# Weight chunks' low halves in parts, roots in two parts, router items ahead of the scores

## What is computed

```
xn = layernorm(x)                                  # (4, 512, 256)
q, k, v = xn @ Wq, xn @ Wk, xn @ Wv                # 16, 4, 4 heads of 128
q, k = rope(q) * scale, rope(k) / scale
s = softmax(causal(q @ k.T / sqrt(128))) @ v @ Wo
p = softmax(xn @ gate_w.T); w, idx = top_k(p, 2)
y = sum_e w_e * swiglu(xn @ w_gate_up[e]) @ w_down[e] + swiglu(xn @ shared_gate_up) @ shared_down
out = x + s * silu(y)
```

## Time and profile before

| | us |
|---|---|
| median of 3 runs (lowest, highest) | 685.43 (684.39, 685.63) |
| the profiled execution | 680.79 |
| its span | 678.9 |
| TensorE busy | 648.1 |
| VectorE busy | 545.6 |
| GpSimd busy | 533.9 |
| ScalarE busy | 421.5 |

### The profile page before, as it was taken

The page is one execution under the profiler, slowest core; times in us unless marked ns, Lnnn a source line. Parts: engine busy times, 40 slices in busy tenths (PEclk is TensorE's granted clock), DMA queues, the critical chain, the costliest instruction groups (busy, mean ns, idle before and its releaser), DMA issues.

```text
span 678.9 us, 15700 instructions
## 1 busy us (share of the span) xinstructions
PE 648.1 (95%) x5187; PEld 463.9 (68%) x5187; DVE 545.6 (80%) x1644; ACT 421.5 (62%) x1157; POOL 533.9 (79%) x609
## 2 busy tenths in 40 slices
PE   8888999999999999999999999999999999999994
PEld 6555677767676677666666766776667777777772
DVE  6999999999999999999899999999875454333356
ACT  5566777776575656666555756557677755555542
POOL 4899898898768787898989898898888974555544
PEclk9999999999999999999999999999999999999998
DMA  9980001011600000000000001000062735676874
GB/s 299 347 235 2 1 1 33 10 25 25 169 1 1 1 1 1 1 18 33 33 24 24 24 24 40 8 32 2 2 101 75 216 64 117 144 152 142 221 285 137
DMA packets 70816, 52.11 MB, mean 77 GB/s; under 512 B 41376, under 2 KB 64128, under 8 KB 70752
## 3 DMA queue, kind: packets, MB, share of 16 engines
q1 hardware_dynamic: 66688, 40.83, 22.8%
q0 software_dynamic: 3792, 10.43, 4.9%
q10 hardware_dynamic: 272, 0.02, 0.0%
HBM read 24.75 MB, written 18.77 MB: 64 GB/s over the span
## 4 chain that ended last, share of the span: by engine, by line
PE 42%; POOL 23%; DVE 19%; issue 8%; ACT 7%; DVEq 0%; ACTq 0%; POOLq 0%
POOL arena L638 11%; PE bank L1753 10%; PE bank L1787 6%; PE bank L1548 5%; PE bank L1608 5%; POOL arena L626 4%; PE bank L1579 4%; PE bank L1625 4%; PE bank L1592 4%; ACT arena L929 3%; POOL xs_dram L697 3%; DVE arena L1267 3%; DVE arena L1240 3%; POOL arena L631 3%; DVE arena L1239 2%
## 5 line engine op out<-in xcount | busy, mean ns | idle before, releaser
L638 POOL TENSOR_TENSOR arena<-arena,rinv 128x64 f32<-128x64 f32 (+7 forms) x256 | 162.4, 666 | 46.8 <-DVE rinv L1261 46.5
L929 ACT ACTIVATE arena<-bank,nmax 128x448 f32<-128x448 f32 (+7 forms) x256 | 125.7, 508 | 49.2 <-DVE nmax L1255 49.0
L937 ACT CAST arena<-bank 128x512 f16<-128x512 f32 (+1 forms) x192 | 94.3, 527 | 42.5 <-PE bank L1592 42.4
L1548 PE MATMUL bank<-xnT_both,arena 128*128 128x512 f16 (+2 forms) x480 | 116.8, 379 | 2.1 <-POOL arena L614 0.8
L1255 DVE CUSTOM_DVE_ANT_0 bank<-bank,mask_b 128x448 f32<-128x448 f32 (+7 forms) x256 | 109.5, 485 | 7.4 <-issue 7.3
L1608 PE MATMUL bank<-arena 128*128 128x512 f16 (+7 forms) x768 | 114.8, 299 | 0.0
L1267 DVE TENSOR_TENSOR arena<-bank,arena 128x512 bf16<-128x512 f32 (+1 forms) x192 | 108.9, 595 | 5.9 <-ACT arena L937 4.8
L1579 PE MATMUL bank<-arena 128*128 128x448 f16 (+15 forms) x768 | 104.7, 286 | 2.7 <-POOL arena L631 1.6
L1592 PE MATMUL bank<-ident_f,arena 128*128 128x128 f32 x640 | 93.1, 276 | 12.1 <-POOL arena L638 9.4
L631 POOL TENSOR_TENSOR arena<-arena 128x512 bf16<-128x512 f32 x80 | 92.8, 1169 | 13.4 <-ACT arena L917 13.3
L626 POOL TENSOR_TENSOR arena<-arena 128x512 f32<-128x512 f32 x79 | 100.2, 1268 | 0.7 <-DVE arena L1240 0.4
(11 more groups left out here) (161 smaller groups left out, 1053.9 us busy)
## 6 DMA issues: line engine op xcount, KB each, us to landing
stage<-w_gate_up SPq DMA_DIRECT2D x16, 352.0 KB
xs_dram<-compare SPq DMA_DIRECT2D x3, 1560.0 KB, 15.7
arena<-ys_dram SPq DMA_DIRECT2D x8, 512.0 KB, 9.1
stage<-w_down SPq DMA_DIRECT2D x16, 176.0 KB
stage<-wq SPq DMA_DIRECT2D x4, 512.0 KB, 9.3
stage<-wo SPq DMA_DIRECT2D x4, 512.0 KB, 9.9
stage<-x SPq DMA_DIRECT2D x1, 2048.0 KB, 10.7
out<-s_sb SPq DMA_DIRECT2D x7, 256.0 KB, 2.1
```

Of the source, the lines that this page charges most:

```text
L638: ins = pool.tensor_tensor(pr, pr, rinv[:, par, qt:qt + 1].to_broadcast([P, n]), ALU.mult)
L929: ins = act.activation(probs[par][:, P_AT[qt]:P_AT[qt] + n], score_bank[u][:, col:col + n], ACT.Exp, scale=-1.0, bias=nmax[:, par, qt:qt + ...
L937: act.copy(pT[j % 2][0][:, at:at + cols], pt_bank[(3 * j + u) % 2][:, 0:cols]).then_inc(pt_hi, 1)
L1548: ins = pe.matmul(ps[:], w[a][:, c * chunk:c * chunk + DH], tokens[m][:, c * TOK:c * TOK + S], start=(c == 0 and n == 0), stop=(c == KC - ...
```

## The change

- `WEIGHTS_AT` names parts now: a chunk, or its half a or b. A half is the columns of two of the four heads in either block of rows. Chunk 3's half a stays on VectorE, its half b goes to GpSimd at round 0, head 1, together with chunk 5. Chunk 4 comes in halves at (0, 2) and (1, 0). TensorE waits by the new counts, with one more wait before the q2 projections of rounds 0 and 1.
- In the prologue VectorE makes the low half of q1 (`second_head_lo`), between the products of q2, and GpSimd does not; chunk 2's low half goes ahead of q2's sum.
- The roots are taken in two parts. Sequence 1 (4 columns): power before the first division, Newton step at round 1, head 2. Sequences 2 and 3 (8 columns): power at round 2, head 0, Newton step at round 2, head 2.
- `normalise(b, half)` waits for one count of `scaled` for sequence 1 and for two for the others, and sequence 1 is normalised one place later, at (1, 3) and (2, 0).
- The fourth router item (`g3`, round 4) and the tile groups (`tile`, round 8) stand ahead of the scores and the q3 projection, no longer at the end of the round.
- `BUSY_SCORE`, the filler before the first scores, is 10 matmuls and no longer 18.

```
-BUSY_PAUSE, BUSY_SCORE = 6, 18
+BUSY_PAUSE, BUSY_SCORE = 6, 10
...
-NORMALISE_AT = {(1, 2): (1, 0), (1, 3): (1, 1), (2, 2): (2, 0), (2, 3): (2, 1), (3, 2): (3, 0), (3, 3): (3, 1)}
+NORMALISE_AT = {(1, 3): (1, 0), (2, 0): (1, 1), (2, 2): (2, 0), (2, 3): (2, 1), (3, 2): (3, 0), (3, 3): (3, 1)}
...
-WEIGHTS_AT = {(0, 1): 4, (0, 2): 5, (1, 1): 6, (1, 3): 7, (2, 3): 8, (3, 3): 9}
+WEIGHTS_AT = {(0, 1): ["3b", "5"], (0, 2): ["4a"], (1, 0): ["4b"], (1, 1): ["6"], (1, 3): ["7"], (2, 3): ["8"], (3, 3): ["9"]}
+WEIGHTS_ORDER = ["0", "1", "2"] + [part for at in WEIGHTS_AT.values() for part in at]
...
-            rotate_lo("q1", PROLOGUE.rot("q1"))
+            weights_lo("2")
             pool.wait_ge(rot_add, PROLOGUE.rot("q1"))
             rotate_sum("q2", PROLOGUE.item("q2"), ROT_BUF_PROLOGUE)
-            weights_lo(2)
+            powers(0)
             divide(0, 0)
...
-                if rd.first and j == 3:
-                    later_powers()
-                if rd.early == 1 and j == 0:
-                    refine_roots()
+                for part in WEIGHTS_AT.get((rd.early, j), []):
+                    weights_lo(part)
+                if rd.early == 1 and j == 2:
+                    refine_roots(0)
+                if rd.early == 2 and j == 0:
+                    powers(1)
+                if rd.early == 2 and j == 2:
+                    refine_roots(1)
...
-                act.wait_ge(scaled, 1)
+                act.wait_ge(scaled, min(b, 2))
...
+            def second_head_lo():
+                dve.wait_ge(rot_hi, PROLOGUE.rot("q1"))
+                dve.tensor_tensor(rotated(1, "q1"), by_half(rot_a[ROT_BUF_PROLOGUE["q1"]]), rotated(0, "q1"), ALU.subtract).then_inc(rot_lo, 1)
...
+                if rd.first:
+                    pe.wait_ge(w_lo, low_parts("3b"))
+                if rd.early == 1:
+                    pe.wait_ge(w_lo, low_parts("4b"))
```

More of the change, by code:

```diff
@@ L423, in w_stage, with w_part, low_parts @@
             return stage[:, n % NSTG * SCOLS:(n % NSTG + 1) * SCOLS]
+        def w_part(ap, half):
+            if not half:
+                return ap
+            side = "ab".index(half)
+            return ap.rearrange("p (c n) -> p c n", c=KC)[:, :, side * GH * DH // 2:(side + 1) * GH * DH // 2]
+        def low_parts(part):
+            return WEIGHTS_ORDER.index(part) + 1
         X_TILES = (slice(0, QT), slice(QT, 2 * QT), slice(2 * QT, NT))
-        LATER = slice(QT, NT)
+        LATER = (slice(QT, 2 * QT), slice(2 * QT, NT))
         SCATTERED = 16 * TOP_K * NT
@@ L644, in split_lo, with powers @@
                 pool.tensor_tensor(lo, xn_t[:, token_tiles(b), :], hi, ALU.subtract).then_inc(rows_lo, 1)
+            def powers(part):
+                at = LATER[part]
+                pool.wait_ge(mask_zero, 2)
+                pool.wait_ge(var_ready, part + 2)
+                pool.tensor_tensor(rstd[:, at], var[:, at], power[:, at], ALU.pow).then_inc(rooted, 1)
             def clear_sum(b):
@@ L674, in expert_lo, with refine_roots @@
                 ins.then_inc(expert_low, 1)
[L676 to L683, removed]
+            def refine_roots(part):
+                at, done = LATER[part], 5 * part
+                v, r, inv = var[:, at], root[:, at], rstd[:, at]
+                pool.wait_ge(rooted, part + 2)
                 pool.tensor_tensor(r, inv, inv, ALU.mult).then_inc(newton, 1)
-                pool.wait_ge(newton, 1)
+                pool.wait_ge(newton, done + 1)
                 pool.tensor_tensor(r, r, v, ALU.mult).then_inc(newton, 1)
-                pool.wait_ge(newton, 2)
+                pool.wait_ge(newton, done + 2)
                 pool.tensor_scalar(r, r, -0.5, 1.5, ALU.mult, ALU.add).then_inc(newton, 1)
-                pool.wait_ge(newton, 3)
+                pool.wait_ge(newton, done + 3)
                 pool.tensor_tensor(inv, inv, r, ALU.mult).then_inc(newton, 1)
[L691 to L694, removed]
+                pool.wait_ge(newton, done + 4)
+                pool.tensor_tensor(shift[:, at], mv[:, at, 0], inv, ALU.mult).then_inc(newton, 1)
+                pool.wait_ge(newton, done + 5)
+                pool.tensor_scalar(shift[:, at], shift[:, at], -1.0, None, ALU.mult).then_inc(scaled, 1)
             def scatter(t, n):
@@ L1227, in tile_groups, with rotate_products @@
                 dve.tensor_copy(group_u[:], misc_bank[rd.bank("tile")][0:1, 0:E_GROUPS]).then_inc(misc_free, 1)
-            def rotate_products(name, item, bank_n, freed, inverted_head=None, bufs=ROT_BUF, late=False):
+            def rotate_products(name, item, bank_n, freed, inverted_head=None, bufs=ROT_BUF, late=False, between=None):
                 ps, buf = misc_bank[bank_n], bufs[name]
@@ L1236, in rotate_products @@
                 half = DH // 2
+                if between is not None:
+                    between()
                 if inverted_head is not None and not late:
@@ L1298, in _ @@
             first_sum("q1")
-            first_rope("q2", PROLOGUE.rot("k"))
+            first_rope("q2", PROLOGUE.rot("k"), between=second_head_lo)
             dve.wait_ge(const_cast, 2)
@@ L1400, in round_ @@
                 routing(rd, 3)
+                if (rd.early, 3) in LOGITS_AT:
+                    logits(rd, LOGITS_AT[rd.early, 3])
+                if rd.early == 8:
+                    tile_groups(rd)
                 if not rd.last:
@@ L1684, in round_ @@
                 weigh_values(rd, 2)
+                if (rd.early, 3) in LOGITS_AT:
+                    router(rd, LOGITS_AT[rd.early, 3])
+                if rd.early == 8:
+                    group_tiles(rd)
                 if not rd.last:
@@ L1690, in round_ @@
                     project_out(rd, 3)
[L1691 to L1694, removed]
             round_(Round(0, "first"))
             for n in range(1, LOOP_FROM):
-                pe.wait_ge(w_lo, WEIGHTS_BY[n])
+                pe.wait_ge(w_lo, low_parts(WEIGHTS_BY[n]))
                 if n == NKV - 1:
```

46 lines of the change are left out of this document (22 added, 24 removed).

## The result

The changed kernel takes **691.4 us** (median of 6 runs, 689.68 to 693.5), the kernel before 684.72 (6 runs, 682.98 to 685.63): a ratio of 1.0099, with the 95% interval 1.0078 to 1.0121, or 6.7 us more. The forecast was 690.7, which is 5.3 us more.

The account below looks back on a forecast made before the run. TensorE, busy 95% of the span, was taken as the bound, its arrival in rounds 0 to 2 moving the end. 1.8 + 1.1 + 3.6 − 0.2 − 1.0 = +5.3 us on 685.43 gave 690.7, range 687.8 to 693.5.

Parts of the forecast that it names:

- the two waits: Round 0: GpSimd waits for ScalarE's chunk 5 high half, +2.9 us; round 2: ScalarE waits for GpSimd's roots, +3.6.
- Step 1: Prologue: with q1's low half on VectorE, the first inverse sums come 0.7 us earlier (bounds 0 to 0.95).
- Step 2: Round 0, head 1: GpSimd waits for chunk 5's high half, +2.9 us; 1.1 comes back, +1.8 after round 1.
- The lower bound: Rounds 0 and 1: all 3.05 us of idle time behind the stall comes back, leaving −0.2 us.
- Step 3: Round 2, head 0: the 8-column power of 1.55 us, less 0.43 of waiting, delays GpSimd's division, +1.1 us.
- Step 4: Round 2, head 2: ScalarE's normalisation waits for GpSimd's root steps, making TensorE's q2 projection late, +3.6 us.
- Step 5: Router items ahead of the scores: fourth logits give −0.2 us, tile groups −1.0.
- Case (a): TensorE's clock falls in the new gap before 47.0 us: about +2 us, 692.7; chance 0.12.
- Case (b): One of the two waits stays off the path: 687.1 to 688.9 us; chance 0.12.
- Case (c): Faster: chunk 5's high half ready when GpSimd asks; with both waits gone −1.6 us, 683.8; chance 0.06.
- Case (d): The whole change does nothing to the time; excluded, with no chance given.

Follow-up runs that it names:

- after: The changed kernel as first run and profiled, with the whole change against the kernel before: 691.4 us, ratio 1.0099.
- after_again: The changed kernel measured once more, unedited, beside the kernel before: 689.7 us, ratio 1.0084.
- no_wait_1: The changed kernel with chunk 5's low half placed behind its high half on GpSimd, ScalarE's wait in round 2 kept: 686.67 us, ratio 1.0039.
- no_wait_2: The changed kernel with sequence 2's normalisation one head later, so ScalarE asks for the second count of roots later; round 0's wait kept: 686.59 us, ratio 1.0035.
- wait_1_alone: The kernel before with only the low halves of chunks 4 and 5 changed round on GpSimd: 688.4 us, ratio 1.0071.
- no_waits: The changed kernel with chunk 5's low half behind its high half and sequence 2's normalisation one head later: 682.58 us, ratio 0.9975.
- eps_on_gpsimd: no_waits with chunk 4's second half at (0, 2), chunk 5 at (0, 3), 8-column power at (1, 1), and the 8-column addition on GpSimd: 682.2 us, ratio 0.9956.
- power_0_late: no_waits with the 8-column power moved to round 1, head 1 and the 4-column power to round 0, head 3: 678.83 us, ratio 0.9966.

## Why the prediction was right

**The mechanism** was right in both places: the two waits stand where they were forecast, with the releasers named, and taking them away takes the slowdown away. In round 2 one link was not named: TensorE first stops for VectorE's low halves of the probabilities (1.91 us, line 1287) and only then for the bank of q2 (0.37 to 1.38 us in after, after_again and no_wait_1, line 1260). Both hang on ScalarE's late casts, so the sum did not suffer.

**Step 1 (prologue, -0.7): too good.** The first inverse sums come 0.3 us earlier, counted from the first transposes (27.57 less 9.12 against 27.68 less 8.93), since VectorE now waits 0.40 us for ScalarE's exponentials, and the division 0.04, since the power, 26.58 for 1.50 us (estimate 0.8), ends only then. To the transposes of head 0 it is 21.32 us against 21.37: 0.05 gained.

**Step 2 (wait 1, +2.9 at R0 h2, of which 1.1 comes back).** Counted from TensorE's first transposes, the delay is 3.3 at R0 h2, and at R1 h1 2.06 in no_wait_2, where the clock stayed (forecast +1.8): the gap was 3.57 us (forecast 3.7), and the 0.7 of the prologue was missing. What comes back between the two is 1.27 us (forecast 1.1, in parts of 0.25, 0.2 and 0.65; measured 0.23, 0.46 and 0.58). The sum came out, the wording did not. The stall itself gives nothing back: in wait_1_alone it is whole at the end, and no_wait_2 stands 3.59 behind no_waits at R0 h2 and 3.57 at R1 h1. In the first GpSimd's own queue carries it on, in the second each later division waits for VectorE's sums (0.70 and 1.32 us), and these shift with TensorE. What comes back is GpSimd's shorter work at the end of round 0 and in round 1: 1.25 us in no_waits, without the wait, and 1.27 with it. The lower bound, in which all idle time of the earlier trace rows swallowed the stall, is what wait_1_alone speaks against.

**Step 3 (8-column power, +1.1 from 1.55 less 0.43).** Measured 1.67, and 1.17 between R1 h1 and R2 h1 in no_waits.

**Step 4 (wait 2, +3.6).** Measured 3.55. (The 1.23 us of the sum are the distance to the next start; its row says 1.27, which changes nothing.)

**Step 5 (-0.2 and -1.0).** The landmarks from R3 h0 to the last give 1.0 to 1.4 together, in all kernels with the change, the fourth logits 0.45 of it (R3 h0 to round 5, head 2, 74.91 us in no_waits against 75.36), more than twice the forecast, and the tile groups the rest, less than forecast.

**The rivals.** Case (a), the clock, had 0.12, and its sign was there in both profiles of the changed kernel; it was not a case apart but comes on top of the forecast, in some executions. Its price was put at 2 us; in the two profiles of the changed kernel it is 3.6 and 0.7 for both gaps. By the medians each gap costs some 0.5 us more than its wait (4.0 to 4.1 against 3.55). That is within the noise, about 1 us for such a difference, but the runs of no_wait_2 say the same: four of twelve, 1.6 us longer. The argument against it, that the only fall in the trace came 4.4 us after the last matmul, was no ground to hold 3.57 us for safe. Nor did I look at round 2, where it fell with no idle stretch above 1.91 us. The Trainium skill, "TensorE: Matmul & The Clock Gate", section "Why this matters for your kernels", warns of too long a pause between bursts; the fall in round 0 agrees, and the one in round 2, behind several short pauses, goes beyond it. Case (b) fell: both waits count whole. Case (c) put the kernel without waits at 1.6 under before; it measured 1.5. Case (d) fell.

**The total.** The measured terms are 2.0 + 1.2 + 3.55 - 1.1 = 5.65 us where the forecast had 5.3; with an estimated 0.5 for the clock at either gap, 6.65. Measured were 6.7 and, in after_again, 5.6, so the share of the clock is not known to better than 1 us. Some of the closeness is luck: the 0.7 that the prologue did not give is in part made up for by a smaller stall (3.36 us, where the forecast's 2.9 and 0.7 make 3.6) and by 0.2 more that came back, and the forecast stands 0.7 lower and not 1.4, because it was laid on the median of three runs, 685.43, and six runs gave 684.72.

## What to carry to other kernels

When a step is moved ahead on one queue, look up where its input is made on the other, and compare the two times before anything else: both losses here were visible in the old trace, to a few tenths. An idle stretch further on pays a stall back only if what ends it is not itself held up by the stall. And tiny instructions in a thin place can be the dear ones, by what stands beside them.

## What the runs showed of the hardware

- **VectorE shut out by GpSimd.** The 8-column addition took 0.17 us with GpSimd all but idle and 1.95 beside GpSimd's low half, and ended at 57.75 where that ended at 57.73. The Trainium skill, "SBUF — State Buffer", section "Who interferes with whom", says that the two share a port pair by an exclusive lock, and that whichever is second can stand still until the first is done. The trace agrees, and eps_on_gpsimd bears it out.
- **GpSimd's power** costs 1.07 us for 4 columns (power_0_late), 1.67 for 8 and 2.32 for 12: some 0.16 per column and 0.45 besides, where a multiplication of 8 takes 0.20. In the prologue the same 4 columns took 1.50, beside a subtraction of VectorE's; that it was the port there too was not tried.
- **The clock after a gap** is not fixed by the gap: with 3.57 us idle it fell in three profiles (after, after_again, wait_1_alone, at 0.50 to 0.69 in the windows from 48 to 52 us) and not in no_wait_2. What decides it stays open.
